# Local attention: the probabilities are divided on GpSimd, the mix puts features on partitions, and the second half of a tile moves back a step

## What is computed

```python
h = shift_token(x)                       # the upper half of the features comes from the token before
q, k, v = split(h @ wqkv)                # 8 heads of 64
q = l2norm(q) * q_scale ; k = l2norm(k) * k_scale
q, k = rotary_xpos(q, k)
sim  = einsum('id,jd->ij', 8 * q, k)     # inside a window of 64 tokens, masked where j > i
attn = softmax(sim)
x = x + einsum('ij,jd->id', attn, v) @ wo
```

## Time and profile before

| | us |
|---|---|
| three runs | 4561.98, 4570.37, 4570.56 |
| median | 4570.37 |
| the profiled execution, its own time | 4563.37 |
| its span, first to last instruction | 4561.6 |
| busy in the span: TensorE 80%, weight loads 52%, VectorE 63%, ACT 41%, GpSimd 31% | |
| mean granted TensorE clock, share of full speed | 0.892 |

### The profile page before, as it was taken

How to read it: one execution, slowest core, us unless ns; L and a number is a source line. 1 busy time by engine, 2 the same in 40 slices (tenths; PEclk the granted TensorE clock), 3 DMA queues, 4 the chain that set the end, 5 groups by cost and what they waited for, 6 DMA issues and landing times. The chain is left out here.

```text
span 4561.6 us, 95626 instructions
## 1 busy us (share of the span) xinstructions
PE 3651.8 (80%) x31569; PEld 2350.1 (52%) x31569; DVE 2882.0 (63%) x6293; ACT 1862.3 (41%) x3725; POOL 1395.2 (31%) x1775
## 2 busy tenths in 40 slices
PE   5676299999788497016995999787999898999897
PEld 5444145454566332015664665554666554666654
DVE  3798811111477769887886676566777544777654
ACT  1233222222477416434552222554666423666521
POOL 0676300000133005432441000005767303767500
PEclk9999599999899698558995999558999999999998
DMA  3111000000000000000110000200000000000000
GB/s 95 38 41 33 26 0 0 0 0 0 13 14 13 6 0 0 0 0 26 45 41 15 1 0 0 93 0 23 9 9 9 6 0 20 9 9 9 9 0 37
DMA packets 121910, 73.93 MB, mean 16 GB/s; under 512 B 57172, under 2 KB 117592, under 8 KB 120792
## 3 DMA queue, kind: packets, MB, share of 16 engines
q1 hardware_dynamic: 120376, 72.41, 5.7%
q10 hardware_dynamic: 1440, 0.34, 0.0%
HBM read 60.18 MB, written 4.19 MB: 14 GB/s over the span
## 5 line engine op out<-in xcount | busy, mean ns | idle before, releaser
L2179 POOL TENSOR_TENSOR la_turned<-la_turned,la_sines 128x1024 f32<-128x1024 f32 x128 | 301.9, 2359 | 694.5 <-DVE la_sines L2105 694.5
L790 DVE TENSOR_TENSOR l0f_y<-A,l0f_s 128x512 f32<-128x512 f32 x16 | 11.1, 692 | 463.4 <-PE A L757 463.4
L2173 POOL TENSOR_TENSOR la_scaled<-la_turned,la_rlen 128x1024 f32<-128x1024 f32 x128 | 243.7, 1904 | 17.1 <-POOL la_rlen L2166 13.7
L1948 PE MATMUL A<-l1f_wT,l1f_down_oq 128*128 128x128 f32 x384 | 54.5, 309 | 225.4 <-DVE l1f_down_oq L1909 225.4
L1057 POOL COPY l1x_vd<-half 128x16 f32<-128x16 f32 x8 | 1.2, 213 | 651.0 <-POOLq L47 651.0
L2403 ACT ACTIVATE gg_gate<-B,gg_b 128x512 f32<-128x512 f32 (+1 forms) x96 | 65.8, 686 | 280.8 <-PE B L2434 280.8
L2075 ACT ACTIVATE la_sq<-A 128x1024 f32<-128x1024 f32 x128 | 131.2, 1025 | 106.8 <-PE A L2225 81.9
L2097 DVE TENSOR_TENSOR la_turned<-A,la_cos 128x1024 f32<-128x1024 f32 x128 | 155.7, 1216 | 29.1 <-issue 15.0
L1948 PEld LDWEIGHTS A<-l1f_wT,l1f_down_oq 128*128 128x128 f32 x384 | 51.9, 220 | 229.0 <-DVE l1f_down_oq L1909 214.8
L2059 ACT ACTIVATE la_prob<-la_prob 128x512 f32<-128x512 f32 x128 | 80.7, 630 | 204.1 <-DVE la_prob L2118 204.1
L2115 DVE TENSOR_REDUCE la_top<-B 128x8 f32<-128x512 f32 x128 | 88.6, 692 | 108.2 <-PE B L2238 108.2
(11 more groups left out here) (447 smaller groups left out, 10680.0 us busy)
## 6 DMA issues: line engine op xcount, KB each, us to landing
memory_ctx<-in_ctx SPq DMA_DIRECT2D x128, 64.0 KB, 2.2
l2x_ctx<-in_ctx SPq DMA_DIRECT2D x128, 64.0 KB, 2.2
X<-in_x SPq DMA_DIRECT2D x4, 1024.0 KB, 8.0
gates_ctxT<-in_ctxT SPq DMA_DIRECT2D x16, 256.0 KB, 2.8
memory_ctxT<-in_ctxT SPq DMA_DIRECT2D x64, 64.0 KB, 1.8
l1x_ctxT<-in_ctxT SPq DMA_DIRECT2D x64, 64.0 KB
l2x_ctxT<-in_ctxT SPq DMA_DIRECT2D x64, 64.0 KB
l3x_ctxT<-in_ctxT SPq DMA_DIRECT2D x8, 512.0 KB, 4.2
```

What stands on the lines that cost most here:

```text
L1948: last = pe.matmul(banks[j][0][:, t * P:t * P + P], oq[j][:, o, t * P:t * P + P], wT[:, 2 * F + o], start=(o == 0), stop=(o == F - 1))
L2173: pool.tensor_tensor(by_head(scaled), by_head(turned), spread_heads(rlen[j % 2][:], W3), ALU.mult)\
L2179: pool.tensor_tensor(turned[j % 2][:], turned[j % 2][:], sines[j % 2][:], ALU.add)\
```

## The change

It moves the division: the sums are taken on VectorE from the probabilities (`totals`), and GpSimd multiplies the probabilities by the inverse in place (`even`). The mix takes v as the stationary side and the probabilities as the moving side, so its result has features on partitions and is copied straight to `oT`; turn_o, the tile `o` and the column of ones are gone. `wo` is loaded in four parts, to match the halves on which the features lie. On TensorE turn_p and mix go from lag -1 to -2 and project from -2 to -3, behind mix; on ACT copy_p -1 to -2, exps 0 to -1, copy_o -2 to -3, and root stands at the head of a step at lag 1 instead of at the end at lag 2; on VectorE add goes from -2 to -4, behind cosines; on GpSimd even stands between rotate and floor.

```diff
+        loads = [(tile[:], src) for tile, src in loads]
+        for half in range(2):
+            for u in range(2):
+                loads.append((wo[half * S:half * S + S, 2 * u:2 * u + 2],
+                              d["l3f_wo"][layer][u * S:u * S + S, (u + half) % 2:G:2]))
-        vd = [st.sb(f"vd{j}", [P, 2, G, W3 + 1]) for j in range(4)]
+        vd = [st.sb(f"vd{j}", [P, 2, G, W3]) for j in range(4)]
-        out = banks(used)[:, :, 0:G * (W3 + 1)].rearrange("p u (g w) -> p u g w", g=G)
-        turned_o, projected = used[:, 0:CH], used[:, CH:CH + P]
+        out = banks(used)[:, :, 0:2 * P].rearrange("p u (g q) -> p u g q", g=2)
+        projected = used[:, CH + 2 * P:CH + 3 * P]
...
                 def copy_o(it, j):
-                    act.wait_ge(o_turned, done(it, j))
+                    act.wait_ge(mixed, done(it, j))
                     act.wait_ge(out_done, done(it, j, 2))
-                    act.copy(oT[j % 2][:].rearrange("p g q -> p (g q)"), turned_o).then_inc(o_copied, 1)
+                    act.wait_ge(added, done(it, j, 1))
+                    act.copy(oT[j % 2][:].rearrange("p (u g) q -> p u g q", u=2), out).then_inc(o_copied, 1)
...
-                    at4(it, j, -1, copy_p)
-                    at4(it, j, -2, copy_o)
+                    at4(it, j, -2, copy_p)
+                    at4(it, j, -1, exps)
+                    at4(it, j, -3, copy_o)
                     at4(it, j, 4, copy_h)
                     at4(it, j, 1, values)
-                    at4(it, j, 0, exps)
                     at4(it, j, 3, squares)
-                    at4(it, j, 2, root)
...
-                def outputs(it, j):
-                    dve.wait_ge(mixed, done(it, j))
-                    dve.reciprocal(inv[j % 2][:], out[:, :, :, W3]).then_inc(inverted, 1)
-                    dve.wait_ge(inverted, done(it, j))
-                    dve.wait_ge(o_turned, done(it, j, 2))
-                    dve.tensor_tensor(o[j % 2][:].rearrange("p (g u w) -> p u g w", g=G, u=2), out[:, :, :, 0:W3],
-                                      inv[j % 2][:, :, :, None].broadcast_to([P, 2, G, W3]), ALU.mult)\
-                       .then_inc(o_done, 1)
+                def totals(it, j):
+                    dve.wait_ge(exped, done(it, j))
+                    dve.tensor_reduce(total[j % 2][:], prob[j % 2][:].rearrange("p g u k -> p (g u) k"), AX, ALU.add)\
+                       .then_inc(totalled, 1)
+                    dve.wait_ge(totalled, done(it, j))
+                    dve.wait_ge(evened, done(it, j, 2))
+                    dve.reciprocal(inv[j % 2][:], total[j % 2][:]).then_inc(inverted, 1)
...
                     at4(it, j, 2, cosines)
+                    at4(it, j, -4, add)
                     at4(it, j, 2, sine_terms)
                     at4(it, j, 0, shift)
-                    at4(it, j, -2, add)
+                    at4(it, j, -1, totals)
                     at4(it, j, 2, lengths)
-                    at4(it, j, -1, outputs)
...
+                def even(it, j):
+                    p = prob[j % 2][:].rearrange("p g u k -> p (g u) k")
+                    pool.wait_ge(inverted, done(it, j))
+                    pool.tensor_tensor(p, p, spread_heads(inv[j % 2][:], S), ALU.mult).then_inc(evened, 1)
...
                     at4(it, j, 2, rotate)
+                    at4(it, j, -1, even)
                     at4(it, j, 2, floor)
...
                 def turn_p(it, j):
-                    pe.wait_ge(exped, done(it, j))
+                    pe.wait_ge(evened, done(it, j))
+                    pe.wait_ge(shifted, ahead(it, j, 1))
...
                 def scores(it, j):
-                    pe.wait_ge(p_copied, done(it, j, 1))
+                    pe.wait_ge(p_copied, done(it, j, 2))
+                    pe.wait_ge(shifted, done(it, j, 1))
...
                 def mix(it, j):
                     pe.wait_ge(v_kept, done(it, j))
-                    pe.wait_ge(added, done(it, j, 1))
+                    pe.wait_ge(o_copied, done(it, j, 1))
                     pe.wait_ge(p_copied, done(it, j))
                     pe.sem_inc(tiles_free, 1)
-                    for g in range(G):
+                    for pair in range(G // 2):
                         for b in range(2):
-                            for u in range(2):
-                                r, c = slice(u * S, u * S + S), slice(b * S, b * S + S)
-                                last = pe.matmul(out[c, u, g], pT[j % 2][r, g, c], vd[j][r, b, g],
-                                                 start=True, stop=True)
+                            for g in (2 * pair, 2 * pair + 1):
+                                for u in range(2):
+                                    r, q = slice(u * S, u * S + S), slice(b * S, b * S + S)
+                                    half = (u + g) % 2
+                                    last = pe.matmul(out[half * S:half * S + S, u, pair, q], vd[j][r, b, g],
+                                                     pT[j % 2][r, g, q], start=True, stop=True)
...
                     at4(it, j, 0, turn_qk)
-                    at4(it, j, -1, turn_p)
-                    at4(it, j, -2, turn_o)
+                    at4(it, j, -2, turn_p)
                     at4(it, j, 1, make_v)
                     at4(it, j, 4, turn_h)
                     at4(it, j, 0, scores)
-                    at4(it, j, -2, project)
                     at4(it, j, 3, make_qk)
-                    at4(it, j, -1, mix)
+                    at4(it, j, -2, mix)
+                    at4(it, j, -3, project)
```

More of the change, by code:

```diff
@@ L1973, in local_attention @@
         loads = [(wq, d["l3f_wq"][layer]), (wk, d["l3f_wk"][layer]), (wv, d["l3f_wv"][layer]),
-                 (wo, d["l3f_wo"][layer]), (cos, d["c_cos"]), (sin, d["c_sin"]), (by, d["l3f_scale"][layer]),
+                 (cos, d["c_cos"]), (sin, d["c_sin"]), (by, d["l3f_scale"][layer]),
                  (by_swapped, d["l3f_scale_swapped"][layer])]
+        loads = [(tile[:], src) for tile, src in loads]
[3 more added lines that the diff above has]
+                              d["l3f_wo"][layer][u * S:u * S + S, (u + half) % 2:G:2]))
         hs, hT = ([st.sb(f"{n}{j}", [P, P]) for j in range(4)] for n in ("hs", "hT"))
@@ L1980, in local_attention @@
         qkT = st.two("qkT", [P, 2, G, P])
-        vd = [st.sb(f"vd{j}", [P, 2, G, W3 + 1]) for j in range(4)]
+        vd = [st.sb(f"vd{j}", [P, 2, G, W3]) for j in range(4)]
         prob, pT = st.two("prob", [P, G, 2, S]), st.two("pT", [P, G, P])
[L1983 to L1986, removed]
+        top, total, inv = st.two("top", [P, 2, G]), st.two("total", [P, HEADS3]), st.two("inv", [P, HEADS3])
+        oT = st.two("oT", [P, G, P])
+        loaded, ready, zeroed, tiles_free, lengths_seen = (
+            st.sem(n) for n in ("loaded", "ready", "zeroed", "tiles_free", "lengths_seen"))
         h_in = [st.sem(f"h_in{j}") for j in range(4)]
@@ L1990, in local_attention @@
          rotated, qk_turned, q_copied, qk_copied, v_made, v_kept, scored, max_done, shifted, exped, p_turned, p_copied, mixed,
-         inverted, o_done, o_turned, o_copied, out_done, added) = (
+         totalled, inverted, evened, o_copied, out_done, added) = (
             st.counter(n, BEFORE) for n in (
@@ L1995, in local_attention @@
                 "scaled_qk", "cosed", "sined", "rotated", "qk_turned", "q_copied", "qk_copied", "v_made", "v_kept", "scored",
-                "max_done", "shifted", "exped", "p_turned", "p_copied", "mixed", "inverted", "o_done", "o_turned",
+                "max_done", "shifted", "exped", "p_turned", "p_copied", "mixed", "totalled", "inverted", "evened",
                 "o_copied", "out_done", "added"))
@@ L2014, in _ @@
                 for tile, src in loads:
-                    sp.dma_start(tile[:], src).then_inc(loaded, 16)
+                    sp.dma_start(tile, src).then_inc(loaded, 16)
                 def shift_in(it, j):
@@ L2022, in shift_in @@
                         sp.dma_start(hs[j][b + 1:b + S, S:P], y[b:b + S - 1, t, S:P]).then_inc(h_in[j], 16)
-                sp.wait_ge(ones_set, 8)
+                sp.wait_ge(zeroed, 4)
                 def step(it, j):
@@ L2063, in values @@
                     act.wait_ge(mixed, done(it, j, 4))
-                    act.copy(vd[j][:, :, :, 0:W3], made_v.rearrange("p (b g w) -> p b g w", b=2, g=G))\
-                       .then_inc(v_kept, 1)
+                    act.copy(vd[j][:].rearrange("p b g w -> p (b g w)"), made_v).then_inc(v_kept, 1)
                 def copy_h(it, j):
@@ L2077, in _ @@
                 act.preload_act_table_set("natural_log_exp_and_others")
-                act.wait_ge(ones_set, 8)
                 def step(it, j):
+                    at4(it, j, 1, root)
                     at4(it, j, 0, copy_qk)
-                    at4(it, j, -1, copy_p)
-                    at4(it, j, -2, copy_o)
+                    at4(it, j, -2, copy_p)
+                    at4(it, j, -1, exps)
```

(8 more changed lines are left out.)

5 lines of the change are left out of this document (1 added, 4 removed).

## The result

| | us, median (lowest to highest), runs |
|---|---|
| before | 4564.85 (4561.98 to 4570.56), 12 |
| after | 4581.59 (4574.37 to 4587.07), 12 |
| ratio | 1.0031, 95% interval 1.0022 to 1.0040 |
| profiled execution after | 4582.71, span 4580.9 (before 4563.37, span 4561.6) |

The kernel is slower by 0.31%, 16.7 us between the medians. The forecast was 4581.0, but the closeness flatters it: I had started from a median of three runs, 5.5 us above that of twelve, and had forecast a change of +10.6, 6.1 us short.

What follows compares the result with a forecast made beforehand. TensorE's ring, waiting for the q copy, was taken to stay the bound at 7.45 us a step. Loads 1.4, fill 0.6 and drain 3.3 make 5.3 a layer, twice +10.6, on 4570.4: 4581.0 us, range 4563 to 4606.

Steps and rivals of the forecast that it cites:

- +10.6: Sum over both local-attention layers: loads, fill and drain cost 5.3 us each layer; the steady part gains nothing.
- TensorE's ring: Steady step: TensorE's repeating cycle, with make_v waiting for the q copy, stays the bound at 7.45 us.
- that chain (1.13 + 0.59 + 0.17 = 1.89) holds nothing that was removed: Steady step, transposes to q copy to make_v: 1.89 us without turn_o, so removing turn_o's 0.47 gains nothing.
- GpSimd's ring: Steady step: floor, refine, scale, rotate, even (1.04) and floor again, priced at 7.39 us, below TensorE's 7.45.
- rival B: GpSimd becomes the bound if even takes 1.10 us or more; 4603 or 4666; sign: GpSimd never idle; chance 0.15.
- Rival C: Steady step: q copy, released by root not TensorE, if its 7.27 us cycle grows by over 0.18; 4593; chance 0.10.
- the ring over scores and totals: Steady step: q copy, make_v, scores, shift, totals, lengths, floor, root, q copy; priced at 7.27 us, not binding.
- Rival D: TensorE's chain shortens: mix to project under 0.56 us instead of 0.62; 4569 at pace 7.35, 4559 at 7.27; chance 0.15.
- Pace 7.45: Steady part: transposes to transposes stay at 7.45 us per step, so it neither gains nor loses.
- Loads (+1.4): Start of each layer: three more wo issues on SP at 0.47 us delay the first matmul by 1.4 us.
- Filling (+0.6): First steps of each layer: the second q copy follows after 7.1 to 7.3 us instead of 6.41; 0.6 us more.
- Drain (+3.3): End of each layer: a tile leaves one step later, +2.6 us, and tail steps without make_qk add 0.7.

Runs made afterwards that it cites:

- experiment 6: The kernel before with one of turn_o's four transposes, the other three left out: 4555.59 us, ratio 0.9977.
- experiment 2: The kernel after with lengths ahead of shift and totals on VectorE, and floor ahead of rotate and even on GpSimd: 4563.02 us, ratio 0.9992.
- experiment 4: The kernel after with project one step later, in TensorE's gap behind turn_p, and add behind the sine terms: 4582.13 us, ratio 1.0037.
- experiment 5: The kernel after with GpSimd's division done twice, first into a buffer nobody reads: 4704.52 us (two runs), ratio 1.0302.
- experiment 1: The kernel after with wo laid out on the host and loaded in one DMA instead of four: 4574.55 us, ratio 1.0021.
- experiment 10: The kernel after with unused identity transposes on TensorE, placed only where it waits in the drain: 4573.87 us, ratio 1.0019.
- experiment 9: The kernel after with eight identity transposes ahead of each turn_p, mix and project in the three steps behind the last tile: 4582.45 us, ratio 1.0030.
- experiment 8: The kernel after with wo in one DMA, lengths and floor early, project in TensorE's gap and turn_p behind project: 4527.01 us, ratio 0.9912.

## Why the prediction came out as it did

*TensorE's ring (7.45 before and after): wrong.* The step that failed is "that chain (1.13 + 0.59 + 0.17 = 1.89) holds nothing that was removed". I read the 0.17 as the time from the copy's end to make_v, since the row names the copy as releaser. It was 0.05; the other 0.12 were turn_o (experiment 6). In the new order project's tail delays the q copy by 0.05 (1.18 behind the loads for 1.13), which leaves 7.36 (experiment 2). turn_o was worth 0.12 in two steps of four and 0.05 in the others.

*GpSimd's ring (7.39): listed among the rings, priced 0.07 short.* even took 1.044, as priced from the nearest form.

```profile
L2193 POOL TENSOR_TENSOR la_prob<-la_prob,la_inv 128x512 f32<-128x512 f32 x128 | 133.7, 1044 | 20.5 <-DVE la_inv L2137 20.5
```

But floor starts 1.13 behind even's start, and refine to scale is 1.38, not 1.30; scale and rotate give back 0.05 each. With TensorE at 7.36 the ring of 7.46 binds (experiments 2, 4, 5). So rival B's threshold of 1.10 was set against the wrong opponent: it was already passed at 1.04. What bound the kernel after is what rival B describes, to which I had given 0.15. Its sign, no idle GpSimd, was too narrow: the ring runs over ACT's root, for which GpSimd idles 0.58. By the Trainium skill's "GPSIMD Engine Reference" (§3.1) even would have taken 1.11; the trace does not agree, 1.044. That page's rule on shared ports (§8) would have kept it at the undisturbed time beside reduces; it runs mostly beside the reduce of lengths and takes the 1.044 of its nearest form, so the trace agrees as far as it goes: no operation with two SBUF inputs runs beside it in the step shown.

*Rival C, the q copy behind root: its sign came, its mechanism did not.* The copy is no longer released by TensorE. But lengths starts at 3412.30, so by the 1.41 of the earlier trace rows floor could have started at 3413.71, and started at 3413.99: 0.28 of room in the ring over scores and totals. I should have seen that B's ring passes through the same root and shows the same sign.

*Rival D, mix faster: it did not happen.* mix to project takes 0.63, as before. TensorE's chain did shorten, elsewhere. D's prices for paces of 7.35 and 7.27 also went below the 7.39 at which my own sum had GpSimd's ring stop it, so the chance of 0.10 for "faster" had nothing to stand on.

*Pace 7.45: near enough by offset.* It was the mean of the steps that counted, 7.51 before and 7.46 after. I read one step of 7.44; the longer one at each turn of the loop, 7.75, I had not looked at.

*Loads (+1.4): under-sized.* 1.94 and 2.05, since a piece of wo takes 0.66 to issue (experiment 1).

*Filling (+0.6): under-sized.* +2.2 and +1.7 in the first four steps. The second step came to 7.37, as the steady ring has it, but the next two took 8.57 and 7.78 (7.45 and 7.52 before). In the first of them make_v ran at 1.2 GHz. In experiment 1 it did not, and the first four steps sum to 28.87 and 28.68, against 29.95 and 29.46: the low clock in that one step was 1.1 and 0.8. The other 1.1 and 0.9 are the longer ring from the second step on; in experiment 2, with the same loads and the same code on TensorE but floor ahead, that step takes 6.04. The same program does both: in experiment 9, whose code up to the drain is that of the kernel after, the step takes 8.57 in la0 and 7.38 in la1.

*Drain (+3.3): the chain nearly right, the clock left out.* At full clock the drain is 17.05 behind the q copy, 3.2 more than before, where I had 2.6 (experiment 10). The steps without make_qk ahead of it took 0.1 more, not 0.7. That the two add up to 3.3 again is luck. The step that failed is that I priced each TensorE operation by its steady rows, in a stretch where TensorE waits more than before. It measured +7.0 and +4.5.

*The sum.* +10.6 forecast, +15.1 measured in the two layers: loads 1.2, filling 2.7 and drain 4.9 too small, the first q copy +0.9 not foreseen (it scatters: 20.7 to 22.3 behind the first matmul in la0 for the same code), the steady part 5.2 too dear. The direction held, and slower was the likeliest of the three cases. The mechanism of the steady part did not hold, and that the sum came out near is luck: the gain there, which I had put at nothing, made up for about half of what the ends cost above their price.

## What to carry to other kernels

A releaser in brackets names what came last by the semaphores, not what filled the time: compare the wait with the same hand-over elsewhere before calling an operation hidden. When work leaves one engine for another, write the rings of both again by start-to-start distances, and look for a small operation (here floor) behind the new one that a third engine waits for; moving it ahead was worth 18 us where the change itself had cost 17. Price a longer drain with the clock in mind, and fill only waits: the same filler gained nothing when it stood ahead of work that was ready.

## What was not expected of the hardware, and what stays open

The clock fell to 0.55 of full in a stretch in which TensorE was still busy 9.86 of 14.60 us, while it held 0.97 in the drain before, at 9.94 of 15.00. The durations after are inflated by the low clock itself, so the two shares don't compare as work; experiment 10 shows only that it stayed up with transposes in the waits. In the filling the same code kept the full clock in some layers and not in others (experiment 9), and what decides it is open. Two DMA issues with the same queue and the same destination tile differ, 0.66 with a piece of wo and 0.54 with the whole (0.48 in the kernel before, where another whole tile follows).

Open: what decides whether the clock falls; whether the kernel before would gain from project in its gap too, which wasn't tried; and what bounds experiment 8 at 7.07. TensorE is the likeliest, busy 198.85 of 200 us with no wait for another engine, where GpSimd is busy 177.91 and waits 3.4 for VectorE; but no run shortened TensorE's work there.
